# Moving the logit exponentials behind the wide tanh, the Newton steps of both norms to GpSimd, and x to the front of the load queue

## The chip, the cores and the metric

One core of a Trainium2 chip runs one program. The metric is the device time of one execution in microseconds (us), lower is better. Engines are named as the profile names them: PE is TensorE, with PEld for its weight loads; DVE is VectorE; ACT is ScalarE; POOL is GpSimd; SP is SyncE, which only issues transfers here.

## What is computed

x has 16 batches of 768 tokens with 128 channels. Three blocks follow each other, each added to its input:

```
x = x + L0_conv(_gn(x))        # group norm, then 8-head attention with two relative biases and a causal mask
t = t + L1_attn(_ln_t(t))      # layer norm, then additive attention:
    hidden = tanh(A[:, :, None, :] + B[:, None, :, :])    # 768 x 768 x 16 per batch
    logits = einsum(hidden, w2) + b2;  attn = softmax(logits);  attn @ v
t = t + L1_ffn(_ln_t(t))       # layer norm, then top-2 of 8 experts with a capacity, 128 -> 512 -> 128
```

## The kernel before, in words

The batches run through a software pipeline of five stages: "pre" (load x, group norm, q, k, v), "max" (row maxima of the scores), "mid" (scores, softmax, values, projection, the sum x1, its layer norm, and A, B, V of the second attention), "add" (the tanh work of the additive attention) and "end" (the layer norm of the result x2, the gate, the choice of experts and the sending of rows). A pass works on five batches at once, one per stage, and is cut into 24 ticks; a tick has four slots. Passes that have all five stages are a loop of 12 passes, two to an iteration; before and behind them stand shorter ones, of which the last four lack "pre", then "max", then "mid", then "add". After the last pass the experts run by themselves.

The order on every engine is written out by hand, from the same tables. `tick_order` (line 114) gives PE and DVE the order in which three PSUM banks, the ring, are filled by PE and read by DVE: PE's `fill` (L1045 on) waits with `pe.wait_ge(ring_read, count)` for the read two uses back. Engines wait for each other by semaphores alone, each in its own program order, so that whatever stands behind a waiting instruction on its engine waits too.

The parts that the change touches:

- **ACT** (`body`, L943 on), in each tick: two exponentials of scores (`exp_scores`, L933), then the wide tanh over three query groups (L956, behind POOL's sums), then the narrow tanh (L962), which releases PE's `add_logits` (L1037). In ticks 5, 9, 13, 17 and 21 the exponentials of the logits of a finished block of 128 queries (`exp_logits`, L940) come too. They wait for `max1_ready`, which DVE sets (L1496, L1498) once PE has added the fourth part of the block. In passes with "mid" they stand ahead of the wide tanh, in others between wide and narrow. PE's first `add_logits` of the next block waits for them (`probs1_ready`), since it overwrites the logits. The sixth block of a batch is treated in tick 1 of the next pass, ahead of the wide tanh.
- **POOL** (`body`, L869 on), in each tick: three sums (L837) into one of four slots of `hidden`, so that it may run ahead of PE by that much; in tick 20 `norm_scale` (L847 to L853), the Newton steps of the first layer norm's inverse root, 12 small instructions; in ticks 18 to 23 and 0 to 5 of a full pass one indirect transfer of rows each (`send`, L866).
- **DVE** (`body`, L1474 on): the reads of the ring, in the order of the ticks. The second layer norm (of x2) and the group norm share one vector of seven variances; seed and three Newton steps of it are `norm_scale(1, k)` in DVE's program at `NORM_AT`, ticks 4, 5, 5 and 6 (L1194 to L1201). Their result is used by `normed(1, ...)` (L1266) in tick 6, by six instructions in two groups of three, and by `xnT` (L1508) in tick 7.
- **SP** (`body`, L684 on): all plain loads and stores, in one queue. `store_block` (L639 to L648) waits for DVE to have read the use "attended" of its block, then stores a block of x2; the fifth block's store stands at the end of a pass. `load_x` (L604), six transfers of 64 KB for the batch of "pre", stands at the start of the next one.
- **PE** (`fill`): the uses A, B and V of "mid" wait for DVE to have copied both halves of x1T (`after("x1T", 1)`).

## Time and profile before

| | |
|---|---|
| Median of 3 runs | 2311.79 us (2310.83 to 2315.6) |
| The profiled execution's own time | 2323.02 us |
| Its span in the trace | 2321.2 us |
| Busy in the span: PE, DVE, ACT, POOL | 89%, 69%, 73%, 65% |
| A pass of the loop | some 120 to 121 us |
| Granted TensorE clock, mean | 0.969 of full speed |

How to read it: the durations come from the one profiled execution. "Idle before" is the time in which an engine did nothing just before an instruction, with the instruction of another engine (or the transfer) that ended it. "Issue" is idle time that ended for no reason that the profile shows. In a timeline a row is one instruction or a run of like ones, with its start and its length in us.

### The profile page before, as it was taken

What the parts mean: (1) busy time and instruction counts of PE and PEld (TensorE: products, weight loads), DVE (VectorE), ACT (ScalarE), POOL (GpSimd) and SP (SyncE); (2) the same over time, 40 slices, a digit from 0 to 9 for tenths busy, and PEclk for the clock granted to TensorE, in tenths of its full rate; (3) what the DMA queues carried; (4) which work ended last, traced back from release to release, by engine and by line L of the source; (5) the groups of instructions that cost most, each with busy time, mean ns of one, the idle gap of its engine ahead of it and who ended that gap; (6) DMA issues with size and microseconds to landing.
All of it is one profiled execution on the core that took longest, in us unless ns stands there. A gap on an engine that the chain in (4) does not pass through costs nothing.

```text
span 2321.2 us, 59625 instructions
## 1 busy us (share of the span) xinstructions
PE 2069.1 (89%) x19525; PEld 1205.1 (52%) x19525; DVE 1601.4 (69%) x4309; ACT 1684.1 (73%) x1934; POOL 1519.7 (65%) x1735
## 2 busy tenths in 40 slices
PE   3889999999999999989998989999999978889996
PEld 2555555555554545455554545454555443458775
DVE  7787786868777777778786878686867554424443
ACT  4449887878887888878787888787888988624332
POOL 5117667576766667666767575757576878737777
PEclk7899999999999999999999999999999998999998
DMA  3746321322222323232323232313131000025553
GB/s 97 123 83 145 82 47 56 57 55 52 64 54 65 56 62 58 62 59 61 57 60 61 56 62 48 68 26 77 33 70 30 12 6 5 25 47 86 88 86 36
DMA packets 157506, 138.14 MB, mean 60 GB/s; under 512 B 24665, under 2 KB 149814, under 8 KB 157104
## 3 DMA queue, kind: packets, MB, share of 16 engines
q1 hardware_dynamic: 119376, 109.87, 22.9%
q0 software_dynamic: 23824, 16.85, 5.3%
q10 hardware_dynamic: 13968, 7.30, 1.3%
q8 instruction: 165, 2.70, 0.5%
q14 instruction: 173, 1.42, 0.2%
HBM read 82.68 MB, written 54.52 MB: 59 GB/s over the span
## 4 chain that ended last, share of the span: by engine, by line
PE 42%; DVE 18%; issue 13%; DVEq 9%; POOL 7%; POOLq 4%; ACT 3%; DMA 3%; SPq 2%; ACTq 0%
PE logits L1037 12%; POOL out_dram L590 4%; PE av_bank L1023 4%; PE ring L1137 4%; DVE max_halves L1310 4%; PE ring L1115 4%; PE scores L1007 3%; PE scores L1010 3%; PE ring L1129 3%; POOLq L836 2%; POOL hidden L837 2%; ACT hidden L956 2%; SPq L604 2%; PE ring L1134 1%; PE ring L1100 1%
## 5 line engine op out<-in xcount | busy, mean ns | idle before, releaser
L837 POOL TENSOR_SCALAR hidden<-b_rep,a_cols 128x768 f32<-128x768 f32 x1152 | 1054.9, 920 | 524.0 <-PE logits L1037 292.3
L956 ACT ACTIVATE hidden<-hidden 128x2304 f32<-128x2304 f32 x384 | 816.2, 2126 | 12.1 <-POOL hidden L837 12.1
L1037 PE MATMUL logits<-hidden,w_shifted 128*32 128x384 f32 x6144 | 586.5, 500 | 60.2 <-ACT probs L940 25.4
L933 ACT ACTIVATE probs<-scores 128x512 f32<-128x512 f32 (+1 forms) x768 | 394.4, 547 | 277.5 <-PE scores L1010 274.9
L1310 DVE TENSOR_REDUCE max_halves<-ring 128x4 f32<-128x512 f32 (+1 forms) x704 | 451.0, 659 | 117.6 <-PE ring L1115 117.2
L962 ACT ACTIVATE hidden<-b_rep,a_cols 128x768 f32<-128x768 f32 x384 | 358.5, 934 | 0.0
L1037 PEld LDWEIGHTS logits<-hidden,w_shifted 128*32 128x32 f32 x6144 | 163.2, 110 | 294.3 <-issue 237.7
L1115 PE MATMUL ring<-k_max,q_max 112*128 112x128 bf16 x2688 | 272.0, 224 | 15.4 <-DVE max_halves L1310 11.6
L1007 PE MATMUL scores<-bias_q,onehot_k 112*128 112x512 bf16 (+1 forms) x768 | 275.8, 360 | 4.1 <-DMA q_parts<-max_parts 2.2
L1010 PE MATMUL scores<-q_parts,k_parts 98*128 98x256 bf16 (+1 forms) x1536 | 277.1, 262 | 0.0
L1115 PEld LDWEIGHTS ring<-k_max,q_max 112*128 112x128 bf16 x2688 | 182.1, 99 | 157.4 <-issue 57.3
L866 POOL DMA_INDIRECT expert_rows<-rows,slots x198 | 201.7, 1019 | 59.2 <-issue 37.7
L1023 PE MATMUL av_bank<-probs,v_aug 128*32 128x256 f32 (+1 forms) x3072 | 223.0, 362 | 11.5 <-DVE headsT_raw L1482 10.5
L1010 PEld LDWEIGHTS scores<-q_parts,k_parts 98*128 98x128 bf16 x1536 | 153.1, 100 | 89.9 <-issue 18.5
L940 ACT ACTIVATE probs<-logits,logit_bias 128x768 f32<-128x768 f32 x96 | 86.6, 902 | 107.7 <-DVE logit_bias L1498 105.9
L517 ACT ACTIVATE hidden<-scores,eb1T 128x384 f32<-128x384 f32 x80 | 46.5, 581 | 162.8 <-PE scores L478 160.1
L1137 PE MATMUL ring<-v,probs1T 128*128 128x128 f32 x1152 | 151.2, 282 | 10.9 <-DVE max_halves L1310 9.2
L1137 PEld LDWEIGHTS ring<-v,probs1T 128*128 128x128 f32 x1152 | 138.9, 194 | 24.1 <-DVE max_halves L1310 18.5
L1368 DVE COPY probs1T<-ring 128x384 f32<-128x384 f32 x192 | 101.7, 550 | 43.7 <-PE ring L1134 43.6
L1007 PEld LDWEIGHTS scores<-bias_q,onehot_k 112*128 112x128 bf16 x768 | 78.0, 102 | 96.0 <-issue 65.4
L489 PEld LDWEIGHTS logits<-probs,hidden 128*128 128x128 f32 x960 | 113.4, 192 | 12.5 <-issue 2.2
L1023 PEld LDWEIGHTS av_bank<-probs,v_aug 128*32 128x32 f32 x3072 | 70.0, 108 | 87.7 <-issue 56.0
(272 smaller groups left out, 2665.1 us busy)
## 6 DMA issues: line engine op xcount, KB each, us to landing
qk_parts<-qk_parts_sb SPq DMA_DIRECT2D x16, 1152.0 KB, 4.5
q_parts<-qk_parts SPq DMA_DIRECT2D x192, 96.0 KB, 3.1
k_parts<-qk_parts SPq DMA_DIRECT2D x192, 96.0 KB, 4.1
q_max<-qk_parts SPq DMA_DIRECT2D x96, 96.0 KB
k_max<-qk_parts SPq DMA_DIRECT2D x96, 96.0 KB
expert_rows<-clear_row ACTq DMA_DIRECT2D x9, 792.0 KB, 5.4
x_in<-in_x_dram SPq DMA_DIRECT2D x96, 64.0 KB
x<-in_x_dram SPq DMA_DIRECT2D x96, 64.0 KB
```

The source lines that it names most:

```text
L837: last = g.tensor_scalar(hidden[:, q % SLOTS, o, :], b_rep[:, side], 1.0, a_cols[:, side, a_col(q, o):a_col(q, o) + 1], ALU.mult, ALU.add)
L866: pool.indirect_dma_start(rows_dram, bass.IndirectOffsetOnAxis(slots[:, k, tb:tb + 1], 0), rows[:, tb, :], None, bounds_check=E * CAP - 1, ...
L933: s.activation(probs0[:, d % 3, 2 * pair:2 * pair + 2, 0:n_], scores[:, pair].rearrange("p (j l) -> p j l", j=2)[:, :, 0:n_], ACT.Exp) \
L956: s.activation(hidden[:, t % SLOTS, 0:3, :], hidden[:, t % SLOTS, 0:3, :], ACT.Tanh)
L962: s.activation(hidden[:, t % SLOTS, 3, :], b_rep[:, side], ACT.Tanh, bias=a_cols[:, side, col:col + 1]).then_inc(tanh_done, 1)
L1007: mm(bank[:, :, 0:n_], onehot_k[:], bias_q[:, h:h + 2, q0 - P * kb:q0 - P * kb + n_], start=True, stop=False, skip_group_check=True)
L1010: last = mm(bank[:, j, 0:n_], k_parts[0:98, h + j, P * kb:P * kb + P], q_parts[0:98, h + j, q0:q0 + n_], start=False, stop=True, skip_grou ...
L1023: last = mm(av_bank[32 * g:32 * g + 32, q0 - lo:q0 - lo + n_], v_aug[:, side, kb, 4 * quad + g, :], probs0[:, d % 3, g, 0:n_], start=(kb = ...
L1037: last = mm(logits[32 * g:32 * g + 32, half, 0:HALF], w2_shifted[:, k, :], hidden[:, q % SLOTS, g, HALF * half:HALF * half + HALF], start= ...
L1115: last = mm(bank[:, P * j:P * j + P], q_max[:, h + j, P * qb:P * qb + P], k_max[:, h + j, P * kb:P * kb + P], start=True, stop=True)
L1137: last = mm(bank[:, 0:P], probs1T[:, P * kb:P * kb + P], v1[:, ps.side(stage), kb, :], start=(kb == 0), stop=(kb == TB - 1))
L1310: v.tensor_reduce(max_halves[:, h % 4:h % 4 + n_, BLOCK_PAIRS.index((qb, kb))], bank[:, 0:n_ * P].rearrange("p (h k) -> p h k", h=n_), AX. ...
```

## The change

Four edits:

1. ACT: `exp_logits` stands behind the wide tanh and ahead of the narrow one in all passes with "add".
2. The second layer norm's and the group norm's Newton steps move from DVE to POOL, in all passes that have "mid" or "end". DVE makes the seed in tick 4 slot 3, POOL the 12 instructions behind its sums of tick 6, and DVE waits for them ahead of `normed(1, ...)`, whose two groups of three now stand in tick 6 slots 2 and 3 (before: slots 1 and 3), and ahead of `xnT` in tick 7. Passes with "pre" alone or with "max" keep the steps on DVE.
3. SP: the store of the fifth block moves from the end of a pass to tick 1 of the next one, behind `load_x`.
4. PE: each half of A, B and V waits for its own half of x1T.

```diff
-SCALE_AT = 20
+SCALE_AT = (20, 6)
...
-                    if ps.has("end") and t == 4:
-                        store_block(ps, "end", 5)
+                    if ps.has("end") and t in (1, 4):
+                        store_block(ps, "end", 4 + t // 4, ps.base if t == 1 else ps.number(("end", "attended", 5)) + 1)
...
-                        store_block(ps, "add", t // 4 - 2)
-                if ps.has("add"):
-                    store_block(ps, "add", 4)
+                        store_block(ps, "add", t // 4 - 2, ps.number(("add", "attended", t // 4 - 2)) + 1)
...
-            def norm_scale(ps):
-
-                var, y, tmp = (ln_small[:, 0, r, 0:TB] for r in range(3))
-                pool.wait_ge(x1_seeded, ps.batch("mid") + 1)
+            def norm_scale(which, c):
+
+                var, y, tmp = (ln_small[:, which, r, 0:TB + which] for r in range(3))
+                pool.wait_ge(norm_seeded[which], c + 1)
...
-                    if t == SCALE_AT and ps.has("mid"):
-                        norm_scale(ps)
+                    if t == SCALE_AT[0] and ps.has("mid"):
+                        norm_scale(0, ps.batch("mid"))
+                    if t == SCALE_AT[1] and (ps.has("mid") or ps.has("end")):
+                        norm_scale(1, ps.batch("pre") - 2)
...
-                    if ps.has("add") and ps.has("mid") and t >= 5 and t % 4 == 1:
-                        exp_logits(ps.batch("add"), t // 4 - 1)
                     if ps.has("add"):
                         b, side = ps.batch("add"), ps.side("add")
                         act.wait_ge(sums_ready, b * 24 + (t + 1))
                         s.activation(hidden[:, t % SLOTS, 0:3, :], hidden[:, t % SLOTS, 0:3, :], ACT.Tanh)
-                        if not ps.has("mid") and t >= 5 and t % 4 == 1:
+                        if t >= 5 and t % 4 == 1:
                             exp_logits(b, t // 4 - 1)
...
                 elif name in ("A", "B", "V"):
-                    after("x1T", 1)
+                    after("x1T", i)
...
-                        if ps.has("pre") or ps.has("end"):
-                            if (t, slot) in NORM_AT:
-                                norm_scale(1, NORM_AT.index((t, slot)))
+                        if (ps.has("mid") or ps.has("end")) and t == 4 and slot == 3:
+                            norm_seed(1)
+                        elif ps.has("pre") and not ps.has("mid") and (t, slot) in NORM_AT:
+                            norm_step(1, NORM_AT.index((t, slot)))
...
+                            if ps.has("mid"):
+                                dve.wait_ge(norm_scaled[1], ps.batch("pre") - 1)
                             v.tensor_scalar(xnT[:], xT[:], gn_small[:, 0:1], ln_small[:, 1, 1, TB:TB + 1], ALU.subtract,
                                             ALU.mult).then_inc(xn_ready, 1)
...
-                            if t == 6 and slot in (1, 3):
-                                if slot == 1:
-                                    dve.drain()
+                            if t == 6 and slot in (2, 3):
+                                if slot == 2:
+                                    dve.wait_ge(norm_scaled[1], ps.batch("pre") - 1)
                                     dve.wait_ge(rows_sent, 112 + c * 192)
```

How it moves instructions on **ACT**, in a tick of a full pass that closes a block (tick 5, 9, 13, 17 or 21), before and now. L933 is `exp_scores`, L940 `exp_logits`; L956 and L954 are the wide tanh, L962 and L960 the narrow one:

```order
L933 ACTIVATE probs<-scores 128x512 [waits av_done]
L928 REGISTER_ALU
L933 ACTIVATE probs<-scores 128x512 [waits scores_filled]
L939 REGISTER_ALU
L940 ACTIVATE probs,row_sum<-logits,logit_bias 128x768 [waits max1_ready]
L955 REGISTER_ALU
L956 ACTIVATE hidden<-hidden 128x2304 [waits sums_ready]
L962 ACTIVATE hidden<-b_rep,a_cols 128x768
```

```order
L933 ACTIVATE probs<-scores 128x512 [waits av_done]
L928 REGISTER_ALU
L933 ACTIVATE probs<-scores 128x512 [waits scores_filled]
L953 REGISTER_ALU
L954 ACTIVATE hidden<-hidden 128x2304 [waits sums_ready]
L939 REGISTER_ALU
L940 ACTIVATE probs,row_sum<-logits,logit_bias 128x768 [waits max1_ready]
L960 ACTIVATE hidden<-b_rep,a_cols 128x768
```

The exponentials of the logits moved behind one wide tanh; the narrow tanh keeps its place behind both.

On **DVE**, tick 6 of a full pass, from the third Newton step to the use of its result, before and now. L1310 and L1307 read the maxima, L1368 and L1365 copy the transposed probabilities, L1266 and L1263 are `normed`:

```order
L1197 SCALAR_TENSOR_TENSOR ln_small<-ln_small 128x7
L1199 TENSOR_TENSOR ln_small<-ln_small 128x7
L1201 SCALAR_TENSOR_TENSOR ln_small<-ln_small 128x7
L1276 REGISTER_ALU
L1310 TENSOR_REDUCE max_halves<-ring 128x4 [waits ring_filled]
L1317 TENSOR_REDUCE neg_max<-max_halves 128x4 x6
L1320 MEMSET gn_small 128x1
L1515 ISA
L1266 TENSOR_SCALAR rows<-x,ln_mv,ln_small 128x128 [waits rows_sent]
L1266 TENSOR_SCALAR rows<-x,ln_mv,ln_small 128x128 x2
L1276 REGISTER_ALU
L1368 COPY probs1T<-ring 128x384 [waits ring_filled]
```

```order
L1307 TENSOR_REDUCE max_halves<-ring 128x4 [waits ring_filled]
L1314 TENSOR_REDUCE neg_max<-max_halves 128x4 x6
L1317 MEMSET gn_small 128x1
L1273 REGISTER_ALU
L1365 COPY probs1T<-ring 128x384 [waits ring_filled]
L1515 ISA [waits norm_scaled_1]
L1263 TENSOR_SCALAR rows<-x,ln_mv,ln_small 128x128 [waits rows_sent]
L1263 TENSOR_SCALAR rows<-x,ln_mv,ln_small 128x128 x2
L1273 REGISTER_ALU
L1365 COPY probs1T<-ring 128x384 [waits ring_filled]
```

The nine Newton instructions are gone from DVE, and the first copy of the transposed probabilities moved ahead of the first three `normed`, which now wait for POOL.

On **SP**, around the loading of x, before and now. `ring_read` is DVE's word that "attended" was read, L604 loads x, L652 what follows it:

```order
L646 REGISTER_ALU [waits ring_read]
L648 ISA [waits x2_stored]
L648 DMA out_dram<-x 16x8x128
L699 ISA
L604 ISA [waits parts_ready]
L604 DMA x_in<-in_x_dram 128x1x128
L604 ISA
L604 DMA x_in<-in_x_dram 128x1x128
```

```order
L604 ISA
L604 DMA x_in<-in_x_dram 128x1x128
L642 ISA
L646 REGISTER_ALU [waits ring_read]
L648 ISA [waits x2_stored]
L648 DMA out_dram<-x 16x8x128
L652 ISA [waits max_done]
L652 DMA q_max<-qk_parts 16x4x768 x2
```

The store of the fifth block, which waits for "attended" in tick 23, moved behind all six transfers of x.

## Rows read from the trace of the kernel before

**Rows 1.** The page, busy time of each engine over the span

```profile
PE 2069.1 (89%) x19525; PEld 1205.1 (52%) x19525; DVE 1601.4 (69%) x4309; ACT 1684.1 (73%) x1934; POOL 1519.7 (65%) x1735
```

**Rows 2.** Busy time by stretch, one full pass: PE, PEld, DVE, ACT, POOL; clock, DMA

```profile
1035.26:1156.00 120.74, 110.07 (x1122) 62.37 (x1116) 93.08 (x241) 98.31 (x110) 80.48 (x96) 0.99 0.27 58
```

**Rows 3.** Who waited for whom, whole span: us in total, times, longest

```profile
ACT probs L940 <- DVE logit_bias L1498: 105.9, 75, 5.5
...
PE ring L1129 <- DVE headsT L1340: 21.8, 16, 1.5
...
PE ring L1100 <- DMA x_in<-in_x_dram: 21.3, 11, 6.6
...
PE ring L1122 <- DVE probs1T L1368: 16.3, 12, 1.8
```

**Rows 4.** Timeline at a pass's start: SP's last store, x, PE's first use

```profile
1117.17 0.61 SPq L648 DMA_DIRECT2D out_dram<-x  x1
...
1118.12 4.74 SPq L604 DMA_DIRECT2D x_in<-in_x_dram  x6
...
1125.89 0.54 PE L1100 MATMUL ring<-ident,x_in 128*128 128x128 f32 x3 [2.23 <-DMA x_in<-in_x_dram]
```

**Rows 5.** Timeline of ticks 6 and 7: DVE's norm, PE's wait, the product behind

```profile
1149.80 1.74 DVE L1266 TENSOR_SCALAR rows<-x,ln_mv,ln_small 128x128 f32<-128x128 f32 x3 [0.18 <-issue]
...
1152.05 0.65 PE L1122 MATMUL ring<-ident,headsT_raw 128*128 128x128 f32 x4 [1.73 <-DVE probs1T L1368]
...
1153.28 2.77 PE L1137 MATMUL ring<-v,probs1T 128*128 128x128 f32 x12
```

**Rows 6.** Groups of DVE, eight full passes (675.34 to 1639.24): Newton steps

```profile
L1201 DVE SCALAR_TENSOR_TENSOR ln_small<-ln_small 128x7 f32<-128x7 f32 x24 | 16.1, 672 | 1.8
...
L1197 DVE SCALAR_TENSOR_TENSOR ln_small<-ln_small 128x7 f32<-128x7 f32 x24 | 9.4, 390 | 2.1
```

**Rows 7.** Timeline: POOL's 12 Newton instructions; last sum of tick 7 and its tanh

```profile
1089.33 0.20 POOL L847 TENSOR_TENSOR ln_small<-ln_small 128x6 f32<-128x6 f32 x1
...
1093.19 0.20 POOL L853 TENSOR_TENSOR ln_small<-ln_small 128x6 f32<-128x6 f32 x1
...
1142.94 0.91 POOL L837 TENSOR_SCALAR hidden<-b_rep,a_cols 128x768 f32<-128x768 f32 x1 [0.17 <-issue]
...
1148.76 2.14 ACT L956 ACTIVATE hidden<-hidden 128x2304 f32<-128x2304 f32 x1
```

**Rows 8.** Timeline of tick 17: ACT's exponentials, PE's two additions of logits

```profile
1080.17 1.08 ACT L933 ACTIVATE probs<-scores 128x512 f32<-128x512 f32 x2 [2.11 <-PE scores L1010]
...
1081.32 0.90 ACT L940 ACTIVATE probs<-logits,logit_bias 128x768 f32<-128x768 f32 x1
...
1082.64 1.50 PE L1037 MATMUL logits<-hidden,w_shifted 128*32 128x384 f32 x16
...
1085.20 1.50 PE L1037 MATMUL logits<-hidden,w_shifted 128*32 128x384 f32 x16 [0.51 <-ACT hidden L962]
```

**Rows 9.** Timeline of tick 5: ACT's exponentials, PE's two additions of logits

```profile
1140.28 0.90 ACT L940 ACTIVATE probs<-logits,logit_bias 128x768 f32<-128x768 f32 x1 [0.91 <-DVE logit_bias L1498]
...
1141.32 1.50 PE L1037 MATMUL logits<-hidden,w_shifted 128*32 128x384 f32 x16 [0.36 <-ACT probs L940]
...
1144.16 1.50 PE L1037 MATMUL logits<-hidden,w_shifted 128*32 128x384 f32 x16 [0.79 <-ACT hidden L962]
```

**Rows 10.** Timeline of tick 21 in two passes: DVE's copies, PE's products for B

```profile
1099.27 1.01 DVE L1340 COPY headsT<-ring 128x384 f32<-128x384 f32 x2
...
1100.41 0.91 PE L1129 MATMUL ring<-headsT,map_b 128*128 128x384 f32 x2 [1.48 <-DVE headsT L1340]
...
1221.03 1.64 PE L1129 MATMUL ring<-headsT,map_b 128*128 128x384 f32 x2 [1.49 <-DVE headsT L1340]
```

**Rows 11.** Timeline, last passes: tanh behind POOL; DVE's Newton steps, first and last

```profile
1948.25 2.12 ACT L956 ACTIVATE hidden<-hidden 128x2304 f32<-128x2304 f32 x1 [1.22 <-POOL hidden L837]
...
2025.52 0.17 DVE L1197 SCALAR_TENSOR_TENSOR ln_small<-ln_small 128x7 f32<-128x7 f32 x1
...
2027.46 0.17 DVE L1201 SCALAR_TENSOR_TENSOR ln_small<-ln_small 128x7 f32<-128x7 f32 x1
```

More of the change, by code:

```diff
@@ L340, in hybrid_kernel @@
         x1n_ready = sem("x1n_ready")
-        x1_seeded = sem("x1_seeded")
-        x1_scaled = sem("x1_scaled")
+        norm_seeded = [sem(f"norm_seeded_{which}") for which in range(2)]
+        norm_scaled = [sem(f"norm_scaled_{which}") for which in range(2)]
         ab_ready = sem("ab_ready")
@@ L637, in copy_tables, with store_block @@
                 sp.dma_start(k_max[96:112, :, :], cn_wide).then_inc(copies_in, 16)
-            def store_block(ps, stage, s):
+            def store_block(ps, stage, s, read):
                 b = ps.batch(stage)
-                sp.wait_ge(ring_read, ps.number((stage, "attended", s)) + 1)
+                sp.wait_ge(ring_read, read)
                 sp.sem_inc(sp_passed, 1)
@@ L854, in norm_scale @@
                     if step == 2:
-                        last.then_inc(x1_scaled, 1)
+                        last.then_inc(norm_scaled[which], 1)
                     else:
@@ L1511, in body @@
                             c = ps.batch("end")
[L1512 to L1514 removed]
+                            if t == 6 and slot in (2, 3):
+                                if slot == 2:
+                                    dve.wait_ge(norm_scaled[1], ps.batch("pre") - 1)
                                     dve.wait_ge(rows_sent, 112 + c * 192)
[L1516 removed]
+                                for tb in range(3 * (slot - 2), 3 * (slot - 2) + 3):
                                     last = normed(1, x2, rows, tb)
@@ L1551, in body @@
                                 if half.start == 0:
-                                    dve.wait_ge(x1_scaled, ps.batch("mid") + 1)
+                                    dve.wait_ge(norm_scaled[0], ps.batch("mid") + 1)
                                 for tb in range(half.start, half.stop):
```

38 lines of the change are left out of this document (18 added, 20 removed).

## The prediction

> **What bounds the kernel now.** I read the page's busy times first, then one full pass by stretch, then the table of who waited for whom, then timelines around the four places that the change touches. PE is busy 89% of the span [rows 1], and in one full pass 110.07 of 120.74 us, against 98.31 for ACT, 93.08 for DVE and 80.48 for POOL [rows 2]. So PE sets the pass, and only some 10.7 us of a pass can be won or lost as PE's idle time; what other engines wait for is free until it reaches PE. The waits table names three of PE's: for DVE's headsT 21.8 us in 16 times, for x 21.3 in 11, for DVE's copy of the transposed probabilities 16.3 in 12. The largest wait, ACT's 105.9 us ahead of the logits' exponentials [rows 3], isn't PE's: the reader is to see that taking it away brings nothing by itself. The profiled execution took 2323.02 us, 11.2 above the median of 2311.79. The sum is made against its own time, and I carry the difference over to the median unchanged. A measurement of this kernel tells about 0.2% (4.6 us) from no change.
>
> **x ahead of the fifth block's store.** SP's store goes out at 1117.17, when "attended" of tick 23 is read, and x's six transfers only at 1118.12; PE's first use of x then waits 2.23 [rows 4]. Now x goes out as soon as the end of the pass before lets SP reach it, at least the 0.95 between the two rows earlier, and more where the wait for "attended" had held SP. The longest of the 11 waits, 6.6, is the program's first load, which stays: 21.3 - 6.6 = **14.7** in ten passes. Bounds: 9.5 (ten times 0.95) to 14.7. I take 14.7, since nothing but loads stands ahead of x in SP's queue now, and SP has long issued those. The store, 0.61 long, stands behind x; nobody waits for it within a pass.
>
> **Newton steps off DVE.** Nine instructions in three steps leave DVE; beside POOL's sums their ends take 390 and 672 ns [rows 6], 170 when POOL is silent [rows 11]. What DVE gains in all is hidden work; on the path lies the 1.73 us for which PE waits for the copy behind the first three `normed` [rows 5], 16.3 in 12 passes. The copy now stands ahead of them, and DVE arrives two steps earlier: **16.3** gone. Bounds: 0 (it is `normed`, 1.74 long, that makes it late) to 16.3.
>
> **A, B, V by halves.** PE waits 1.48 for the second half's copy [rows 10], though its first product needs the first half alone. DVE's two copies take 1.01 together, so some 0.45, less than the second one's 0.5, of each of 16 waits goes: **7.2**. Bounds: 0 to 16 times 1.0.
>
> **The clock.** After some of these gaps the product behind runs at half speed: 2.77 for a use that elsewhere takes 1.50 behind the gap of rows 5, 1.64 for 0.91 behind one of two like gaps of 1.49 and 1.48 [rows 5, 10]. In the timelines seven of the gaps that go or shrink were followed so. By the 1.27 of rows 5 that is 7 x 1.3 = **9.1**. Bounds: 3 (three of them, where the gap vanishes) to 12. Gains in all: 14.7 + 16.3 + 7.2 + 9.1 = 47.3.
>
> **Exponentials behind the wide tanh.** PE's first addition of the next block waits for them, since it overwrites the logits. In tick 5 ACT is free at 1140.28 - 0.91 = 1139.37 [rows 9]. Now the wide tanh comes first (2.0 to 2.1), then 0.90: the exponentials end near 1142.3 and PE starts near 1142.4, 1.05 later than 1141.32. PE's second addition waited 0.79 for the narrow tanh, which isn't later than before; that wait is used up. Net 0.3. In tick 17 ACT is behind for another reason, the scores that came 2.11 late [rows 8]: it would start the wide tanh at 1081.32 and the exponentials end near 1084.2, so PE starts 1.6 later than 1082.64, of which 0.51 was waited for further on. Net 1.1. In ticks 9, 13 and 21 ACT runs ahead far enough. (0.3 + 1.1) x 15 passes = 21; the first pass with "add", whose ACT has less in front, 2 more. The new waits of 1 to 1.6 are as long as those that dropped the clock; if 4 of them do, 4 x 1.3 = 5. Together **28**. Bounds: 0 (ACT has more lead than in the two ticks shown) to 15 x (1.05 + 1.6) + 10 = 50.
>
> **Newton steps on POOL.** The 12 instructions and the drains between them took 1093.39 - 1089.33 = 4.06 us [rows 7], 0.20 each. Behind the sums of tick 6 they stand in front of the sums of tick 7, the last of which ended at 1143.85, 4.9 ahead of its tanh at 1148.76 [rows 7]; in other passes this lead is 3.2 to 7. So tick 7 is covered. But POOL recovers only slowly: its lead is thinner by 4.06, and sends of rows stand in ticks 0 to 5 ahead of it. I charge 1.2 us, the size of the wait that ACT shows behind POOL where POOL is late [rows 11], in 7 of 12 passes: 8.4. In the pass without "mid" where ACT already waits for POOL [rows 11], all 4.1 counts. In the last pass with "end" nothing else runs: DVE's steps took 2025.52 to 2027.63, 2.1, POOL's would take 4.06 and two handoffs, so 2.1 more. Together **14.6**. Bounds: 6 to 12 x 4.06 + 6 = 55. DVE's new wait ahead of `normed` should be empty: POOL would finish near 1143.85 - 2.75 + 4.06 = 1145.2, and DVE was at `normed` at 1149.80 [rows 5]. Behind it would stand the ring's reads, so were it late, PE would stop two uses on.
>
> First the row, then the rule: an instruction of this norm takes 0.17 on DVE alone and 0.20 on POOL [rows 7, 11], so the two are near each other here. The Trainium skill, GPSIMD Engine Reference, section "Engine selection", speaks against this edit: elementwise work on a tile belongs on VectorE, since GpSimd is some two times slower on two inputs. By that page 12 instructions on POOL would take about twice DVE's time each, an estimate of 12 x 0.34 = 4.1 without drains, and the second rival would gain weight. For the edit speaks the 390 and 672 of rows 6 beside the 170 of rows 11. On these the Trainium skill, SBUF - State Buffer, section "Who interferes with whom", says that VectorE and GpSimd share one port pair under an exclusive lock; the trace agrees in that DVE's steps are two to four times longer beside POOL's sums, and by that rule POOL's own steps would be lengthened in turn by DVE.
>
> Sum: -47.3 + 28 + 14.6 = **-4.7**, so 2311.8 - 4.7 = **2307 us**.
>
> **The rivals.**
> Forecast (0.45): gains and costs nearly balance. Its own range is 2296 to 2318, from the bounds of the clock and of the ticks that pay.
>
> First rival, the exponentials cost nothing (0.20). For it: ACT has 22 us of idle time in a pass [rows 2], and 105.9 us of its waits are ahead of these very exponentials [rows 3]; moving them fills that wait with the wide tanh, so ACT gets ahead by 0.9 in each of these ticks and may stay ahead. Against it: in ticks 5 and 17 PE is at the door already [rows 8, 9]. -47.3 + 14.6 = -33: 2279 us.
>
> Second rival, slower (0.25): POOL's chain decides ticks 7 to 9 of every full pass. The Newton steps take 4.06 of a lead that is 3.2 to 4.9, and ACT, which is now ahead through the first edit, asks for its sums earlier. The price is then midway between 1.2 and 4.06, 2.6 in 12 passes, 31.6 in place of 8.4: +23 on the forecast, +18.5 over before, 2330 us. It decides as soon as POOL's lead ahead of the wide tanh of tick 7 is below 4 us. For it: ACT's wait of 1.22 behind POOL exists in the trace. Against it: POOL is idle 40 us of a pass [rows 2].
>
> Third rival, the wait behind `normed` doesn't go (0.10): both groups of three now stand in neighbouring slots, 1.74 each in front of a copy, and PE waits at the second of them, or DVE waits for POOL. Of the gains 16.3 stay out: +11.6, 2323 us.
>
> **How the numbers follow.** The forecast lies at the edge of what can be told from no change: its 0.45 is split into 0.24 faster, 0.17 the same, 0.04 slower. The first rival is faster (0.20), the second slower (0.25), the third half-way (0.06 slower, 0.04 the same). Faster 0.44, same 0.21, slower 0.35. The range takes in the forecast's own, the third rival, and half of each of the two outer ones, with their bounds of a few us: 2281 to 2331.
>
> **What would show it.** Right: PE's wait for x gone but for the first; no wait on the copy of the transposed probabilities in tick 6; the waits on headsT near 1.0; ACT's idle time ahead of L940 small and PE's wait for it 1 to 1.6 in ticks 5 and 17; hardly any wait of ACT on POOL in ticks 7 to 9 of full passes; DVE's wait for POOL empty; the passes without "mid" and "add" 6 longer together; the same number of half-clock stretches or fewer. Wrong: a pass of the loop shorter by over 2 us (then the exponentials are free), or ACT's waits on POOL's sums over 2 us in each pass, or PE's wait at the ring's read two uses behind `normed`.

## The result, and the profile after

| | before | after |
|---|---|---|
| Median of 5 runs | 2311.79 us (2310.83 to 2317.78) | 2331.6 us (2324.44 to 2336.04) |
| Ratio after to before | | 1.0071, 95% interval 1.0046 to 1.0097 |
| The profiled execution's own time | 2323.02 us | 2324.44 us |

The kernel became slower, by 16 us by the ratio (11 to 22; the medians are 19.8 apart); forecast was 5 us faster. The two profiled executions differ by only 1.4 us. The first kernel's was 5 us above all of its timed runs, the second's is the fastest of its five. So a second trace of the kernel before was taken (2313.74 us, "second trace" from here on), and the stretches below are compared with that one.

The page of the kernel after, busy time of each engine (it answers to [rows 1]):

```profile
PE 2072.1 (89%) x19525; PEld 1209.8 (52%) x19525; DVE 1577.2 (68%) x4147; ACT 1681.9 (72%) x1934; POOL 1564.0 (67%) x1951
```

DVE lost 162 instructions and POOL gained 216, as in the change. Who waited for whom, of the kernel after, whole span (it answers to [rows 3]):

```profile
PE logits L1035 <- ACT probs L940: 71.2, 43, 6.2
...
ACT hidden L954 <- POOL hidden L835: 54.1, 43, 5.7
...
ACT probs L940 <- DVE logit_bias L1495: 30.0, 27, 4.7
...
PE ring L1098 <- DVE heads L1263: 22.2, 15, 6.0
...
PE ring L1127 <- DVE headsT L1337: 14.0, 14, 1.0
...
PE ring L1098 <- DMA x_in<-in_x_dram: 6.5, 1, 6.5
```

The reader is to see that most forecast steps can be found here: the wait for x is gone but for the first load (6.5), the one for the transposed probabilities has left the head of the table, headsT went from 21.8 to 14.0 and is 1.0 at most. ACT's idle time ahead of the exponentials fell from 105.9 to 30.0, and PE's wait for them rose from 25 to 71. One line was in no step: PE's wait for `heads` behind L1263, the rows of the *first* layer norm, for the use x1T. It is 22.2 in sum, and was 15.2 in the first trace of before and 14.6 in the second.

Where the time went is told by four stretches: up to the first full pass, the twelve full passes, the two behind, and the last two with the experts. The windows view of the second trace of before, and of the kernel after (length, then PE, PEld, DVE, ACT, POOL busy; clock, DMA):

```profile
0.00:271.26 271.26, 219.52 (x2069) 129.23 (x2069) 205.84 (x500) 165.93 (x211) 116.15 (x176) 0.92 0.51 108
271.26:1708.42 1437.16, 1320.98 (x13448) 741.31 (x13440) 1102.26 (x2881) 1168.64 (x1310) 964.63 (x1152) 0.99 0.27 57
1708.42:1917.47 209.05, 183.10 (x1814) 98.43 (x1810) 134.15 (x358) 179.11 (x191) 156.81 (x189) 0.96 0.14 23
1917.47:2312.00 394.53, 339.00 (x2214) 235.00 (x2206) 153.87 (x572) 170.94 (x226) 277.07 (x219) 0.95 0.36 55
```

```profile
0.00:277.36 277.36, 222.68 (x2069) 131.67 (x2069) 205.55 (x482) 166.76 (x211) 121.76 (x200) 0.90 0.50 107
277.36:1704.28 1426.92, 1318.57 (x13448) 740.59 (x13440) 1096.02 (x2773) 1163.92 (x1309) 997.92 (x1297) 0.99 0.27 57
1704.28:1916.46 212.18, 183.40 (x1829) 99.58 (x1822) 127.85 (x340) 180.08 (x191) 161.13 (x213) 0.97 0.13 23
1916.46:2322.70 406.24, 347.44 (x2198) 238.01 (x2196) 147.76 (x554) 171.10 (x226) 283.15 (x243) 0.92 0.35 53
```

The twelve full passes became 10.2 us **shorter**. The stretches around them became 6.1, 3.1 and 11.7 longer, 10.7 in all. The change pays where the steady work is and loses more at both ends. A single trace carries noise here: two later pairs of kernels are alike up to the last two passes (after and full_dve_tail, no_exps and best), and in the traces of one pair the full passes differ by 4.0 and what lies ahead of them by 4.1, in the other by 2.6 and 6.1. In the ten kernels whose exponentials of tick 17 are moved, the first stretch took 273.2 to 278.1, in the others 266.4 to 274.1, so some 6 us there (276.9 against 270.8 in the mean) go with that move.

The end first. In the last pass with "end" nothing else is left to do. The timeline of the kernel after there (start, length, engine, line):

```profile
2018.53 0.17 DVE L1244 TENSOR_SCALAR ln_small<-ln_small 128x7 int32<-128x7 int32 x1
2018.89 0.20 POOL L845 TENSOR_TENSOR ln_small<-ln_small 128x7 f32<-128x7 f32 x1 [3.90 <-DVE ln_small L1244]
2019.98 0.20 POOL L847 TENSOR_TENSOR ln_small<-ln_small 128x7 f32<-128x7 f32 x1 [0.89 <-issue]
...
2023.54 0.20 POOL L851 TENSOR_TENSOR ln_small<-ln_small 128x7 f32<-128x7 f32 x1
2023.77 1.63 DVE L1263 TENSOR_SCALAR rows<-x,ln_mv,ln_small 128x128 f32<-128x128 f32 x6 [5.07 <-POOL ln_small L851]
...
2025.46 1.54 PE L1098 MATMUL ring<-ident,rows 128*128 128x128 f32 x6 [3.96 <-DVE rows L1263]
```

and the same place of the kernel before, first trace:

```profile
2027.71 1.63 DVE L1266 TENSOR_SCALAR rows<-x,ln_mv,ln_small 128x128 f32<-128x128 f32 x6
...
2029.39 0.87 PE L1100 MATMUL ring<-ident,rows 128*128 128x128 f32 x6 [1.25 <-DVE rows L1266]
```

DVE waits 5.07 for steps that it did itself in 2.27 (the seed ended at 2025.44, the rows began at 2027.71). Both kernels give PE 14 products that nobody reads to pass this time. Before they left a wait of 1.25; now PE stands still 3.96, and the six transposes behind take 1.54 instead of 0.87: the clock is at half. 2.8 us of serial work so became 8.1 (the stretch behind the last wide tanh, 308.8 before and 316.9 after). All traces below agree: in the four kernels with these steps on POOL the stretch took 316.7 to 318.5, in all others 308.6 to 312.7. In the pass ahead of it POOL's 12 instructions lengthen POOL's chain, 3.6 us.

### The profile page after: what moved, and what is told of

The parts are those of the page before. It is cut to its first block, busy times and chain, and to the rows that moved or that the text cites. A ratio compares the mean times of both kernels' runs of the same rounds, so it can differ in the third digit from the quotient of the medians.

```text
span 2322.7 us, 59745 instructions
## 1 busy us (share of the span) xinstructions
PE 2072.1 (89%) x19525; PEld 1209.8 (52%) x19525; DVE 1577.2 (68%) x4147; ACT 1681.9 (72%) x1934; POOL 1564.0 (67%) x1951
## 4 chain that ended last, share of the span: by engine, by line
PE 43%; DVE 17%; issue 13%; POOL 8%; DVEq 7%; ACT 5%; POOLq 4%; DMA 2%; SPq 0%; ACTq 0%
PE logits L1035 14%; PE ring L1113 4%; PE av_bank L1021 4%; POOL out_dram L590 4%; DVE max_halves L1307 4%; PE scores L1005 4%; POOL hidden L835 3%; PE scores L1008 3%; POOLq L834 3%; PE ring L1135 3%; PE ring L1127 2%; ACT hidden L954 2%; ACT probs L940 2%; PE ring L1132 2%; DVE logit_bias L1493 1%
## 5 line engine op out<-in xcount | busy, mean ns | idle before, releaser
L954 ACT ACTIVATE hidden<-hidden 128x2304 f32<-128x2304 f32 x384 | 817.5, 2129 | 54.2 <-POOL hidden L835 54.1
L933 ACT ACTIVATE probs<-scores 128x512 f32<-128x512 f32 (+1 forms) x768 | 394.2, 548 | 309.7 <-PE scores L1008 307.3
L1307 DVE TENSOR_REDUCE max_halves<-ring 128x4 f32<-128x512 f32 (+1 forms) x704 | 451.1, 660 | 165.6 <-PE ring L1113 163.6
L960 ACT ACTIVATE hidden<-b_rep,a_cols 128x768 f32<-128x768 f32 x384 | 359.5, 936 | 0.0
L1135 PE MATMUL ring<-v,probs1T 128*128 128x128 f32 x1152 | 150.1, 281 | 16.6 <-DVE max_halves L1307 14.6
L1135 PEld LDWEIGHTS ring<-v,probs1T 128*128 128x128 f32 x1152 | 137.6, 193 | 29.9 <-DVE max_halves L1307 23.8
L1365 DVE COPY probs1T<-ring 128x384 f32<-128x384 f32 x192 | 102.9, 551 | 54.6 <-PE ring L1132 54.3
L489 PE MATMUL logits<-probs,hidden 128*128 128x128 f32 x960 | 113.7, 275 | 1.5 <-DVE gn_small L559 1.5
```

The costliest lines, as they stand in the source:

```text
L489: last = mm(logits[:, n % 2, P * b_:P * b_ + P], gelu_out[n % 2][:, j, P * b_:P * b_ + P], down_w[r][:, j, :], start=(j == 0), stop=(j == 3))
L933: s.activation(probs0[:, d % 3, 2 * pair:2 * pair + 2, 0:n_], scores[:, pair].rearrange("p (j l) -> p j l", j=2)[:, :, 0:n_], ACT.Exp) \
L954: s.activation(hidden[:, t % SLOTS, 0:3, :], hidden[:, t % SLOTS, 0:3, :], ACT.Tanh)
L960: s.activation(hidden[:, t % SLOTS, 3, :], b_rep[:, side], ACT.Tanh, bias=a_cols[:, side, col:col + 1]).then_inc(tanh_done, 1)
L1135: last = mm(bank[:, 0:P], probs1T[:, P * kb:P * kb + P], v1[:, ps.side(stage), kb, :], start=(kb == 0), stop=(kb == TB - 1))
L1307: v.tensor_reduce(max_halves[:, h % 4:h % 4 + n_, BLOCK_PAIRS.index((qb, kb))], bank[:, 0:n_ * P].rearrange("p (h k) -> p h k", h=n_), AX. ...
```

## The experiments

Sixteen kernels' traces are compared by three numbers of their twelve full passes, taken from the start of one wide tanh to another: the stretch's length; PE's idle time in it (its length less PE's busy time in the windows view); and the time at half clock, worked out from the windows view in pieces of 1 us as the sum of 2 x (1 - granted clock) where that is under 0.97. The last column counts in how many of the twelve passes such a stretch lies in ticks 20 to 22. The ratio is to runs of the kernel before on the same chip, whose median was 2315.5 to 2322.2 (2311.8 for the change itself). Where a text below says how much slower or faster a kernel is, that is by the ratio, unless it says otherwise.

| kernel | median, us | ratio (95%) | full passes | PE idle | half clock | passes |
|---|---|---|---|---|---|---|
| before, first trace | 2311.8 | | 1443.5 | 117.5 | 40.9 | 4 |
| base | 2316.1 | 0.9994 (0.9976 to 1.0012) | 1437.2 | 116.2 | 30.7 | 4 |
| the change | 2331.6 | 1.0071 (1.0046 to 1.0097) | 1426.9 | 108.4 | 27.3 | 4 |
| exps_only | 2385.4 | 1.0286 (1.0260 to 1.0312) | 1495.2 | 146.4 | 98.9 | 12 |
| newton_only | 2322.3 | 1.0025 (1.0008 to 1.0042) | 1432.9 | 110.9 | 34.0 | 4 |
| x_halves | 2299.8 | 0.9924 (0.9902 to 0.9947) | 1420.5 | 102.2 | 27.3 | 2 |
| exps_halves | 2364.9 | 1.0209 (1.0181 to 1.0236) | 1479.7 | 142.9 | 75.1 | 12 |
| exps_newton | 2345.6 | 1.0125 (1.0097 to 1.0153) | 1448.5 | 120.7 | 47.8 | 6 |
| full_dve_tail | 2321.2 | 1.0021 (1.0002 to 1.0039) | 1430.9 | 108.6 | 37.5 | 6 |
| no_exps | 2299.2 | 0.9927 (0.9901 to 0.9954) | 1413.8 | 95.7 | 23.8 | 2 |
| exps_17 | 2376.2 | 1.0248 (1.0222 to 1.0274) | 1488.0 | 146.2 | 85.3 | 12 |
| exps_rest | 2325.6 | 1.0040 (1.0025 to 1.0055) | 1436.9 | 117.4 | 30.6 | 3 |
| exps_scale19 | 2363.0 | 1.0179 (1.0153 to 1.0206) | 1471.4 | 143.1 | 51.3 | 7 |
| exps_warm | 2366.2 | 1.0202 (1.0175 to 1.0228) | 1476.4 | 135.9 | 40.9 | 5 |
| exps_nonewton | 2350.0 | 1.0119 (1.0086 to 1.0153) | 1467.1 | 131.5 | 68.3 | 9 |
| exps_pool12 | 2361.2 | 1.0165 (1.0136 to 1.0194) | 1468.4 | 131.2 | 75.0 | 9 |
| best | 2288.0 | 0.9863 (0.9838 to 0.9888) | 1411.2 | 93.6 | 23.8 | 2 |

The columns check each other: a us at half clock loses half a us, so the full passes should move by the idle time and half of the half-clock time. For x_halves that is -14.0 - 1.7 = -15.7 against base, measured -16.7; for the change -7.8 - 1.7 = -9.5, measured -10.3; for exps_only 30.2 + 34.1 = 64.3, measured 58.0. It holds within 7 us everywhere but in exps_warm, whose 17.5 us of added products count as busy; with them it holds there within 3.

**The single edits.** The kernel before again (label base), and each edit alone; Newton with its own slots of `normed`, and the two small ones on SP and PE together:

> The kernel before, once more, for a second trace of it. Theory A (the profiled execution of before was one with more half-clock stretches in the loop than its median run): 2312 us, and the twelve full passes take some 10 us less than the 1443.6 of the first trace, with the passes behind them as before (13 and 14: 112 and 97 us). Rival B (the profile itself lengthens every execution by 11 us): again 1443 us for the twelve passes.

Theory A was right in kind: the full passes took 6.4 less than in the first trace, with 10 us less at half clock; the passes behind were as before. The terms of the prediction had been read from an execution with more of it than usual.

> Only the exponentials of the logits moved behind the wide tanh. Theory A (they cost PE what its waits for L940 grew by, 46 us, less the 20 that went from its waits for the narrow tanh, plus 3 us in the first pass with add): 26 to 30 us slower than before, 2338 to 2342. Rival B (in the full passes they are nearly free, and the loss of the whole change sits in the last passes): 2312 to 2318. Rival C (the cost is there only because the other edits took PE's other waits away): 2320 to 2328.

```diff
-                    if ps.has("add") and ps.has("mid") and t >= 5 and t % 4 == 1:
-                        exp_logits(ps.batch("add"), t // 4 - 1)
...
-                        if not ps.has("mid") and t >= 5 and t % 4 == 1:
+                        if t >= 5 and t % 4 == 1:
```

All three theories fell: 66 us slower (2.86%), over twice the largest. PE's idle time in the full passes grew by 30, and the half-clock time by 68.

> Only the Newton steps moved to GpSimd, with the two groups of normalised rows in slots 2 and 3. Theory A (16 us of PE's wait in tick 6 go, 10 to 13 are lost behind the loop, where the steps stand alone on the path and the clock falls): 2306 to 2310. Rival B (GpSimd's thinner lead costs in every full pass): 2325 to 2335, with ACT's waits for GpSimd's sums near 50 us. Rival C (the loss in the last passes is chance): 2294 to 2298.

The median lies in no theory's range: 0.25% slower, some 6 us. The full passes gained 4.3, which is no more than two traces of one kernel differ by; the last two stretches lost 0.5 and 11.6. PE's waits in tick 7, 13.4, were gone as forecast. But those for x1T in tick 20 rose from 5.9 to 12.3: POOL, which does the first norm's Newton steps there, is done with them 0.6 later behind the wide tanh of tick 17 (11.4 against 10.8). ACT's waits for POOL grew only from 13.5 to 29.7 in the whole span, and from 0 to 5.4 in the full passes.

> Only the loads of x ahead of the fifth block's store, and A, B and V waiting for their own half. Theory A (the waits that go, 15 and 8 us, are PE's and nothing takes their place): 2287 to 2291. Rival B (PE then waits elsewhere for the same thing, the engines behind it being as late): over 2300.

```diff
-                    after("x1T", 1)
+                    after("x1T", i)
...
-                    if ps.has("end") and t == 4:
-                        store_block(ps, "end", 5)
+                    if ps.has("end") and t in (1, 4):
+                        store_block(ps, "end", 4 + t // 4, ps.base if t == 1 else ps.number(("end", "attended", 5)) + 1)
...
-                if ps.has("add"):
-                    store_block(ps, "add", 4)
```

18 us faster, 0.76%, with 14.0 us less idle time of PE in the full passes; the wait for x, gone, had been 15.2. Theory A was right on the waits for x and 10 us too hopeful in all: of PE's waits for headsT 5.6 of 17.8 went, and 2.7 came back ahead of x1T.

So singly the edits give +66, +6 and -18, +54 together; the change as a whole costs 16. The exponentials must cost less in the others' company.

**In company.** Two pairs, and the whole change less one part:

> The exponentials behind the wide tanh, and of the other edits only that A, B and V wait for their own half of x1T. The exponentials alone cost 66 us; 12 of 12 full passes then had the clock at half in tick 21, against 4 of 12 without them, behind two waits of PE close together, 2.05 for x1T and 1.48 for headsT. Theory C (the pair of waits drops the clock; with the second one at 1.03 it often stays up): about half of the clock's 30 us come back besides the 6 us of the shorter wait, so 2350 to 2368, with half-clock stretches in tick 21 in at most 7 of 12 passes. Rival D (the first wait of 2.0 alone drops it): 2377 to 2381, again 12 of 12.

> The exponentials behind the wide tanh, and the Newton steps on GpSimd; loads of x and the waits of A, B and V as before. Singly they cost 66 and 6. Theory C (the pair of waits in tick 21 drops the clock): the Newton edit changes nothing there, so 2380 to 2392. Rival E (with the Newton steps off it, VectorE is at the first layer norm's rows early enough that the wait of 2.05 for x1T goes, and with it the clock's loss): 2335 to 2355, with the wait for x1T under 1.2.

> The whole change without the move of the exponentials. The single edits gave +6 and -17. Theory A (they add up): 2303 to 2309. If the exponentials cost 66 us in this company too, the whole change would stand at 2370, which it doesn't: so here they cost 24 to 30. Rival G (the Newton steps on GpSimd hurt only beside the moved exponentials, by taking its lead): 2295 to 2300.

The halves bring the exponentials' cost from 66 down to 48. The time is in the range of theory C, yet the count of passes stayed at 12, as rival D had it: the half-clock stretches became shorter (98.9 to 75.1), not fewer. The Newton edit brings the cost to 29, in the range of rival E: waits for x1T in six of twelve passes only, half clock in six. Without the exponentials the whole change stands at 2299, 17 to 19 us faster than before, though the Newton edit loses 12 of that behind the loop; in that company the exponentials cost 33. The time is rival G's, but its mechanism isn't shown: beside the moved exponentials the Newton edit took 37 us off.

**Which exponentials.** Only those of tick 17 moved, and only the others:

```diff
+                        if t >= 5 and t % 4 == 1 and (t == 17 or not ps.has("mid")):
```

> Only the exponentials of tick 17 stand behind the wide tanh; all else as before. Theory H (tick 17 makes nearly the whole cost of 66: PE's 1.6 late at its addition, POOL's Newton steps of the first layer norm 1.2 later, the rows of that norm then beside POOL's sums, a wait of 2.05 for x1T in tick 21, and the clock at half in 12 of 12 passes): 45 to 58 us slower than before. Rival I (the ticks share it: PE comes late to tick 5, and stays late): 20 to 30.

> The complement: the exponentials of ticks 5, 9, 13 and 21 stand behind the wide tanh, those of tick 17 ahead of it as before. Theory H: 3 us for tick 5 in twelve passes and 3 for the first pass with add, so 4 to 14 us slower than before, the clock in tick 21 at half in no more than 6 passes of 12. Rival I: 30 or more.

Theory H was right on both: 57 us and 9, and twelve passes against three. The waits table of exps_17 and that of the second trace of before, in this order, show that the price isn't mainly in the wait that the move makes:

```profile
PE logits L1037 <- ACT probs L940: 47.7, 39, 6.2
PE ring L1100 <- DVE heads L1266: 32.6, 16, 4.0
```

```profile
PE logits L1037 <- ACT probs L940: 25.2, 25, 6.2
...
PE ring L1100 <- DVE heads L1266: 14.6, 16, 5.5
```

PE's own wait in tick 17 is 1.58 (18.4 in twelve passes, in place of 6.2 behind the narrow tanh), a net 1.0 per pass. The second line is four ticks further on: the rows of the first layer norm, 18 more. The timeline of exps_only at that place, tick 21 of one pass, and then that of the second trace of before:

```profile
998.60 2.59 DVE L1264 TENSOR_SCALAR heads<-x,ln_mv,ln_small 128x128 f32<-128x128 f32 x3
999.20 1.92 POOL L837 TENSOR_SCALAR hidden<-b_rep,a_cols 128x768 f32<-128x768 f32 x2
...
1002.32 1.53 DVE L1264 TENSOR_SCALAR heads<-x,ln_mv,ln_small 128x128 f32<-128x128 f32 x3
1003.99 0.54 PE L1098 MATMUL ring<-ident,heads 128*128 128x128 f32 x3 [1.80 <-DVE heads L1264]
...
1007.05 1.64 PE L1127 MATMUL ring<-headsT,map_b 128*128 128x384 f32 x2 [1.47 <-DVE headsT L1338]
...
1008.91 1.59 PE L1127 MATMUL ring<-headsT,map_b 128*128 128x384 f32 x2
...
1010.72 1.59 PE L1127 MATMUL ring<-headsT,map_a 128*128 128x384 f32 x2
```

```profile
850.54 0.20 POOL L853 TENSOR_TENSOR ln_small<-ln_small 128x6 f32<-128x6 f32 x1
...
850.78 0.86 DVE L1266 TENSOR_SCALAR heads<-x,ln_mv,ln_small 128x128 f32<-128x128 f32 x3
...
852.38 1.84 POOL L837 TENSOR_SCALAR hidden<-b_rep,a_cols 128x768 f32<-128x768 f32 x2
...
852.78 1.77 DVE L1266 TENSOR_SCALAR heads<-x,ln_mv,ln_small 128x128 f32<-128x128 f32 x3
854.69 0.54 PE L1100 MATMUL ring<-ident,heads 128*128 128x128 f32 x3 [0.82 <-DVE heads L1266]
...
857.76 0.91 PE L1129 MATMUL ring<-headsT,map_b 128*128 128x384 f32 x2 [1.48 <-DVE headsT L1340]
858.73 0.86 PE L1129 MATMUL ring<-headsT,map_b 128*128 128x384 f32 x2
```

PE waits 1.8 (2.05 in the mean) for x1T, three us later 1.47 for headsT, and then the products for B and A take 1.6 where they take 0.9: half clock, in tick 21 of every pass. In seven of the twelve passes (six in exps_17, seven in exps_halves) the clock was at half before the second of the two waits began, so the first one, of 1.8 to 2.4 us, needs no second. In the trace of before the two waits are 0.82 and 1.48 here, and the clock mostly stays. Why the rows are late is in the groups view of DVE over the full passes, this line of before (second trace), of exps_only and of the kernel after:

```profile
L1266 DVE TENSOR_SCALAR heads<-x,ln_mv,ln_small 128x128 f32<-128x128 f32 x72 | 29.4, 465 | 0.3
```

```profile
L1264 DVE TENSOR_SCALAR heads<-x,ln_mv,ln_small 128x128 f32<-128x128 f32 x72 | 50.3, 754 | 0.0
```

```profile
L1263 DVE TENSOR_SCALAR heads<-x,ln_mv,ln_small 128x128 f32<-128x128 f32 x72 | 40.5, 617 | 0.0
```

The same instruction takes 465, 754 or 617 ns by what POOL does beside it. The two timelines show where: before, the first three rows fell into the time in which POOL had ended its Newton steps and made no sums yet, and took 0.86; with PE's addition of tick 17 late, POOL's steps end 1.2 later (12.0 against 10.8 behind the wide tanh of tick 17), the rows begin 2.0 later and stand beside POOL's sums, 2.59. The Trainium skill, SBUF - State Buffer, section "Who interferes with whom", says that VectorE and GpSimd share a pair of ports under an exclusive lock. The trace agrees in that the rows take longer beside sums, 754 against 465; the lock itself can't be seen in it.

**The norm earlier, and the clock by itself.** First the first layer norm's Newton steps one tick earlier, beside the moved exponentials (`SCALE_AT = 19`):

> All exponentials behind the wide tanh, and the first layer norm's Newton steps on POOL one tick earlier (19 in place of 20). Theory H (what costs is that this norm comes late to x1T in tick 21): the wait of 2.05 for x1T goes or falls below 1, VectorE's six normalised rows take near 2.5 us again in place of 4.8, the clock is at half in tick 21 in at most 6 passes of 12, and of the 66 us 30 to 45 come back: 2338 to 2355. Rival J (PE's wait of 1.6 in tick 17 and that for headsT drop the clock whatever x1T does): 2362 to 2375. Rival K (POOL now waits for VectorE's seed ahead of its sums of tick 20 and ACT for those): over 2375, with ACT's waits for POOL over 40 us.

25 of the 66 us came back. The median is in J's range, at its lower end; H's signs came half-way: the rows took 634 ns, the wait for x1T fell to 1.37, and the clock was at half in 7 passes. POOL's result was there 2.5 us earlier, but DVE reaches the rows in its own order of slots; POOL's waits for the seed cost ACT 31 us of waiting, as K had it, but the time K forecast from them didn't come.

Then the clock apart from the wait. PE issues products that nobody reads into the free bank, ahead of its wait for x1T:

```diff
                 elif name == "x1T":
+                    if i == 0 and ps.has("end"):
+                        pe.wait_ge(ring_read, ps.number(use) - (RING - 1))
+                        for _ in range(6):
+                            mm(bank[:, 0:512], ones_bf[0:112, :], bias_q[:, 0, 0:512], start=True, stop=True)
                     pe.wait_ge(x1n_ready, c + 1)
```

> The exponentials behind the wide tanh (66 us slower than before), and in passes with all stages PE issues six products of 512 columns that nobody reads into the free ring bank, ahead of its wait for x1T; a like product took 0.27, so 1.6 of the wait of 2.05 are filled. Theory C (the clock falls because PE stands still 2.05 and then 1.48; that is about half of the cost): the clock is at half in tick 21 in at most 4 passes, half-clock time of the twelve passes falls from 99 us to 30 to 45, and 25 to 35 us come back: 2350 to 2360. Rival N (the clock falls there whatever PE does in that wait, or the waits alone are the cost): 2380 to 2390.

The timeline of exps_warm there:

```profile
990.66 1.46 PE L1080 MATMUL ring<-bias_q,ones_bf 112*128 112x512 bf16 x6
...
992.53 0.55 PE L1102 MATMUL ring<-ident,heads 128*128 128x128 f32 x3 [0.41 <-DVE heads L1268]
```

x1T is as late as in exps_only (18.4 behind the wide tanh of tick 17, against 18.5), nothing else was changed, and the half-clock time fell from 98.9 to 40.9, from twelve passes to five; 19 us came back, less than the 25 to 35 of theory C, though the half-clock time is where C had it (30 to 45) and the passes are one more than its four. So at least 19 of the 66 us are the clock, brought down by PE standing still there; the half-clock column puts all of the clock's part at 34. By that column 29 should have come back here; in a pass with full clock some waits are longer than at half, since PE arrives sooner (headsT 13.7 to 18.6).

**Why the Newton edit helps the exponentials.** VectorE relieved without anything on GpSimd, and GpSimd burdened without relief:

> The exponentials behind the wide tanh; of the second norm and the group norm only the seed is computed in passes with mid, the nine Newton instructions are left out (their results are the seed's), and nothing is added on GpSimd. Theory M (VectorE's relief is what makes the move cheaper beside the Newton edit): 2340 to 2355. Theory L (GpSimd's shift does it): 2370 to 2380, less the 13 us of PE's wait in tick 7.

> The exponentials behind the wide tanh; VectorE keeps its Newton steps, and GpSimd does 12 more small instructions behind its sums of tick 6 in passes with all stages, on a tile that nobody reads. Theory L (GpSimd, later by 4 us from tick 6, meets VectorE's rows of tick 19 differently): 2350 to 2365, six rows near 3.3 us instead of 4.8, waits for x1T in half of the passes. Theory M (VectorE's relief): 2385 or more.

Both hit the range of their own theory, 35 and 24 us below exps_only by the medians (39 and 28 by the ratios); the waits for x1T that L forecast in half of the passes came in all, and the rows stayed nearer to exps_only's. So neither is *the* cause; with each alone DVE's rows meet POOL's sums less (664 and 705 ns in place of 754), and with the whole edit, which takes 37 us off, less still (566 ns in exps_newton). Some 11 of exps_nonewton's 35 us are PE's wait of tick 7, which went. The second run had a side result: with POOL's twelve small instructions in tick 6 in place of sums, PE's wait of tick 7 fell from 11.5 to 3.1, though DVE still did all of its Newton steps. The two longest instructions of a step fell from 567 and 393 ns to 314 and 262. Most of that wait had come from DVE working beside sums, not from the number of its instructions.

**The tail, and a faster kernel.** The whole change, and the change without the exponentials (best), each with the Newton steps on DVE in the passes that have no "mid":

```diff
-                    if t == SCALE_AT[1] and (ps.has("mid") or ps.has("end")):
+                    if t == SCALE_AT[1] and ps.has("mid"):
...
-                        if (ps.has("mid") or ps.has("end")) and t == 4 and slot == 3:
+                        if ps.has("mid") and t == 4 and slot == 3:
                             norm_seed(1)
-                        elif ps.has("pre") and not ps.has("mid") and (t, slot) in NORM_AT:
+                        elif (ps.has("pre") or ps.has("end")) and not ps.has("mid") and (t, slot) in NORM_AT:
```

> The whole change, but in the two last passes with end, which have no mid, the second norm's Newton steps stay on VectorE. Theory A (3.6 us of the loss sit in the pass with add and end, 8 in the last one, where the steps in series made a wait of 3.96 and then half clock): 11 to 12 us faster than the whole change, 2318 to 2323. Rival F (the clock falls there anyway, since the chain behind the last exponentials is nearly as long): 2326 to 2330.

> The exponentials where they were; x ahead of the store, A, B and V by halves, the second norm's Newton steps on GpSimd in passes with mid and on VectorE in the last two. Without the last exception it was 19 us faster than before (2299 beside 2318). Theory A (the two last passes lose 11 to the Newton steps on GpSimd): 29 to 31 us faster than before. Rival F (nothing from the tail): 19.

Theory A held in kind twice: by the medians 10.4 us off the whole change and 11.2 off the one without the exponentials, by the ratios 11.6 and 14.8. The second kernel stands at 2287.96 us (2283.68 to 2289.58), 1.4% under the kernel before (1.1 to 1.6%), and beats both kernels. It is 27.5 us faster than before by the medians and 31.7 by the ratio, either side of the forecast 29 to 31. Its windows, full passes and last stretch:

```profile
272.51:1683.68 1411.17, 1317.61 (x13448) 738.55 (x13440) 1083.02 (x2773) 1164.67 (x1309) 997.84 (x1297) 0.99 0.27 58
...
1891.36:2286.40 395.04, 340.01 (x2202) 234.45 (x2200) 154.11 (x572) 171.05 (x226) 278.07 (x219) 0.95 0.35 55
```

## Why the prediction was wrong

The mechanisms were named rightly and most of PE's waits were sized well. Against base, by the prediction's own terms:

| step | forecast | measured |
|---|---|---|
| x, waits of ten passes | -14.7 | -15.2 |
| PE's wait in tick 7 | -16.3 | -13.4 in the full passes |
| headsT by halves | -7.2 | -7.9 (21.9 to 14.0) |
| tick 5, full passes | 12 x 0.3 = 3.6 | 13.8 to 16.2: +2.4 |
| tick 17, full passes | 12 x 1.1 = 13.2 | 6.2 to 18.4: +12.2 |
| first pass with "add" | +3.4 | front stretch +6.1 |
| clock | -9.1 + 5 | half clock 30.7 to 27.3 in the full passes: -1.7 |
| x1T | none | +5.7 in the full passes, +7.6 in all |
| Newton steps on POOL, full passes | +8.4 through ACT | ACT's waits for POOL 0 to 25.8, no new wait of PE behind them |
| Newton steps on POOL, last two passes | +6.2 | +11.7 |

In the full passes the named waits come to -13.9 (headsT's share there is -5.6), and PE's idle time fell by 7.8 only; 3.2 of the rest is PE's wait for the maxima in tick 12 and 2.0 is idle time at a pass's start. By edits, with the ratios: x and the halves -18 (forecast -21.9), the Newton edit on top +1 (-1.7), the exponentials on top +33 (28, with 5 for the clock); that is 16 in all. The forecast's -9.1 for the clock stands in none of these three.

**The steps that failed** are three terms of the sum. The largest is the clock: a gain of 9.1 was booked against a cost of 5, and 1.7 came in the full passes, none in the last stretch, where the granted clock fell from 0.95 to 0.92.

Second, the last passes: POOL's steps were put at 4.06 and two handoffs against DVE's 2.1, so 2.1 more. The chain did grow by 2.8 (the twelve steps took 4.85, since the first two stood 1.09 apart), but it was priced as if PE only arrived later. PE ran out of its passing products, stood 3.96 and came back at half clock, and 8.1 us were lost in that pass. The Trainium skill, GPSIMD Engine Reference, section "Engine selection", which the prediction weighed there, puts elementwise work on VectorE, and that advice was right in this pass: 5.07 us of waiting against 2.27. Its reason, GpSimd's some two times slower instructions on two inputs, isn't what the trace shows: they are 0.20 against 0.17. The chain has twelve in place of nine, spaced by 0.35 against 0.24.

Third, x1T, put at nothing: the cost of the exponentials was followed to PE's next addition of logits and no further. What PE's lateness did to POOL, to POOL's sums beside the first norm's rows, and so to PE in tick 21 was in no term. Alone it made the exponentials cost 66 in place of 28; beside the other edits they cost 33, and the wait itself 5.7 to 7.6. That the forecast for them looks near is in part luck. The 8.4 charged for ACT's waits hid some of it, for PE never paid them.

**The clock term** was wrong in kind. Each gap was given a chance of its own to drop the clock and each drop a price of 1.3. In the runs the drops come behind the waits of some 2 us for x1T and at the start of a pass, now and then behind headsT's alone, and each costs several products, 3.4 or 6.8 us at half clock. The drops were counted in the first trace, whose full passes had 10 us more half-clock time than the second one's, so part of the gain was never there to be had.

**Rival two** (slower, POOL's chain decides ticks 7 to 9) gave 2330 and the time came out at 2331.6, but not by that mechanism. Its condition came true: POOL's last sum of tick 7 ended 0.03 ahead of its tanh in all twelve passes, against 2.6 to 7.8 in the trace that the prediction was read from, so that tick 7 is covered was wrong, and ACT waited there 23.5 in sum. Yet ACT had been made early by the first edit, and those waits don't reach PE; the full passes became shorter. Newton_only, which has no moved exponentials, has 5.4 of them and full passes no longer than before. **Rival one** (the exponentials cost nothing, 2279) is wrong: 33 us in this company. **Rival three** (the wait behind `normed` stays) is wrong: PE's wait in tick 7 is gone in every kernel with the Newton edit.

Left open: why in some passes the clock falls and in others not behind like waits, and what the second wait in tick 21 adds to the first; only the first was filled. And of the change's 16 us the traces account for 10.7; the profiled execution was the fastest of its five, and the others left no trace that would show where they lost 1 to 12 us more.

## What to carry to other kernels

When a step is moved so that an engine comes a little later, follow the lateness past the next wait: to the third engine that waits for the late one, and to whose work that then lies beside. Read a change to a loop at its ends too, where the same few instructions stand alone on the path; there the engine that needs the fewest us from first to last instruction is right, whatever is right in the steady state. And price PE's idle time by its length too: exps_only's waits for x1T grew by 19 us in the full passes, and the half clock cost 34.

## What was unexpected of the hardware

- One instruction of DVE (128x128, f32) took 465 to 768 ns in the mean of 72, by what POOL did beside it (base and exps_halves).
- Waits of 2.05 and 1.15 in the mean, some 1.6 us of products between them, had the clock at half in 12 of 12 passes, in seven of them before the second wait began. With the first filled by products to 0.7 and the second at 1.55, it was in 5 of 12; with waits of 0.49 and 1.48, in 4 of 12.
- The same twelve full passes of the same kernel had 40.9 and 30.7 us at half clock in two traces, and took 1443.5 and 1437.2 us. A single trace of a kernel like this is no better than that.
- Twelve small POOL instructions in place of sums took 8.4 us out of PE's waits of tick 7, without any engine being relieved.
